# Reciprocals and scaling of attention outputs moved from VectorE to GpSimd in 14 of 16 chunks

## The chip, the cores and the metric

The kernel runs on one core of a Trainium2 chip. The metric is device time of the whole kernel in microseconds (us), as the median of several runs. The engines are TensorE (PE; PEld is its weight load), VectorE (DVE), ScalarE (ACT) and GpSimd (POOL); SyncE (SP) issues nearly all DMAs.

## What is computed

The reference is a transformer block with self-attention, cross-attention and a gated feed-forward part, followed by one more attention over the same context. Cut to what matters:

```python
def sdpa(q, k, v):
    probs = jax.nn.softmax(jnp.einsum('bid,bjd->bij', q, k) * SCALE, axis=2)
    return jnp.einsum('bij,bjd->bid', probs, v)

x = attention(ln32(x, ln1_s, ln1_b), ln32(x, ln1_s, ln1_b), Wq1, Wkv1, Wo1, bo1) + x
x = attention(ln32(x, ln2_s, ln2_b), context, Wq2, Wkv2, Wo2, bo2) + x
x = geglu_ff(ln32(x, ln3_s, ln3_b), Wff1, bff1, Wff2, bff2) + x
# second block: softmax((x Wq + bq)(ctx Wk + bk)^T) (ctx Wv + bv) + x
```

x is 4 x 1024 x 256 in float32, the context 4 x 154 x 256; there are 16 heads of 16 columns. Both multi-head attentions divide each head's output by the sum of its exponentials, and this division is what the change is about.

## The kernel before

**Tiling.** The 4096 rows are cut into 16 chunks of 256 (CH). A chunk passes through the stages `pre` (first normalisation, q, k, v), the self-attention (scores, maxima, exponentials, values), `mid` (output projection of the self-attention, residual, second normalisation, q of the cross-attention), `cross` (cross-attention) and `last` (output projection of the cross-attention, residual, third normalisation, feed-forward, final attention, store). The stages work on different chunks at the same time: body n of the main loop runs `pre` of chunk n, `mid` of chunk n - 6, `cross` of n - 7 and `last` of n - 8 beside the self-attention.

**Order.** Every engine has its own program, written as Python generators. The table ORDERS holds one string of letters for each body, and `walk` (L483) goes through it on every engine: each letter takes the next step of one stage or of the attention. All engines so walk the same list of steps; a step issues what that engine does in it, often nothing. Engines work in order and meet through semaphores, so an instruction that waits holds up everything behind it on its engine. The letter `i` stands for the reciprocal of a `last` chunk.

**The division.** The attention's values carry a column of ones, so each head's 17th row of output is the sum of its exponentials. Outputs and sums go to DRAM. In `mid` and in `last` the same six steps follow:

1. SP fetches the sums of 16 heads x 256 rows in packed form into den_c, 128 x 32 (load_den, L685; semaphore c_den).
2. DVE makes their reciprocals in place (invert, L1282; c_rd).
3. SP waits for c_rd and stores them to DRAM (store_inv, L689).
4. SP loads them back, each broadcast over the 16 rows of its head, into den, 128 x 512 (load_inv, L698). The unscaled outputs were loaded into oT before (load_sums, L693).
5. DVE multiplies oT by den in place (norm_o, L1287; c_on).
6. PE waits for c_on and projects (project_rows, L1560), DVE adds the residual (L1293).

Index 0 of these semaphores is `mid`, index 1 `last`. In the trace the second set of tiles carries the same names oT, den, x and xb.

**Work around it.** DVE's largest part is the maxima of the scores, 1024 reductions of 128 x 512 out of PSUM (L1398). In the feed-forward part DVE makes a gate from two SBUF tiles (L1356) and the hidden tile from it (L1359), which PE multiplies next (L1725). POOL makes the reciprocal square roots of the normalisations (L905, L907, an addition and a power with a tile of -0.5, 128 x 2), splits q and k into bfloat16 parts (L914, L916, L918, 128 x 512) and adds biases to the residuals (L935). At the start of `last`, POOL's bias addition to xb waits until the output of the chunk before is stored (c_outst).

Of the kernel before, what the change touches and what calls it, by code (L numbers as in the profile page):

```python
# [8 lines left out]
ALU = mybir.AluOpType  # L9
# [3 lines left out]
P = 128  # L13
B, S, D = 4, 1024, 256
H, DH = 16, 16
# [4 lines left out]
CH = 256  # L20
TT = CH // P
NCH = B * S // CH
# [16 lines left out]
EXPS2 = [name for name in ORDER2 if name[0] != "V"]  # L39
NE2 = len(EXPS2)  # L40
PR = 5
VSLOTS = 2
EPS = 1e-5
SCALE = 64 ** -0.5
# [125 lines left out]
def xattn_kernel(nc, t, out):  # L170

    ctx = ExitStack()
    with ctx:
        def sb(name, shape, dt=F32):
            return ctx.enter_context(nc.sbuf_tensor(name, shape, dt))
# [4 lines left out]
        def sem(name):  # L180
            return ctx.enter_context(nc.semaphore(name))
# [14 lines left out]

        ident = sb("ident", [P, P])
        neghalf = sb("neghalf", [P, TT])
        wq1 = sb("wq1", [P, KD, D])
        wkv1 = sb("wkv1", [P, KD, 2 * D])  # L200
        wo1 = sb("wo1", [P, KD, D])
# [44 lines left out]
        oT = sb("oT", [P, KD, CH])  # L246
        den = sb("den", [P, KD, CH])
# [28 lines left out]
        den_c = [sb(f"den_c{i}", [P, H * CH // P]) for i in range(2)]  # L276
# [68 lines left out]

        s_vec = sem("setup_vectors_loaded")
        s_load = sem("setup_pre_loaded")
        s_load2 = sem("setup_context_loaded")
        s_load3 = sem("setup_rest_loaded")
        s_const = sem("setup_constants")  # L350
# [63 lines left out]
        c_in = sem("mid_in_loaded")  # L414
# [4 lines left out]
        c_den = [sem(f"{c}_den_loaded") for c in ("mid", "last")]  # L419
        c_rd = [sem(f"{c}_inv_den") for c in ("mid", "last")]  # L420
# [429 lines left out]
        def _(pool):  # L850
            nc.gpsimd.memset(ident[:, :], 0.0).then_inc(s_const, 1)
            pool.wait_ge(s_const, 1)
            nc.gpsimd.affine_select(out=ident[:, :], in_=ident[:, :], compare_op=ALU.not_equal, fill=1.0, base=0,
                                    pattern=[[-1, P]], channel_multiplier=1).then_inc(s_const, 1)
            nc.gpsimd.memset(neghalf[:, :], -0.5).then_inc(s_const, 1)
            nc.gpsimd.memset(v_sb[:, :, :, DH:DH + 1], 1.0).then_inc(s_const, 1)
            nc.gpsimd.memset(head_v[1][:, :, :, DH:DH + 1], 1.0).then_inc(s_const, 1)
# [62 lines left out]
            def pre(p):  # L920
# [9 lines left out]
                for _ in range(2):  # L930
                    yield

            def add_bias(dst, x, bias, done):
                for i in range(TT):
                    last = nc.gpsimd.tensor_tensor(dst[:, i, :], x[:, i, :], bias[:, :], ALU.add)  # L935
                last.then_inc(done, 1)

            def mid(o, has_pre):
                yield
                pool.wait_ge(c_x0, (o + 1) * 16)  # L940
                add_bias(x0, x0, bo1, c_xb[0])
                for _ in range(3):
                    yield
                rstd(mv[0], ve[0], rs[0], c_mv[0], c_ve[0], c_rs[0], o + 1)
                for _ in range(3):
                    yield
                pool.wait_ge(c_q2st, o * 16)
                parts(q2_f, q2_parts, PART_AT[0], c_q2f, c_q2hi, c_q2rest, c_q2mid, c_q2lo, o + 1, o + 1)
                yield
                yield  # L950
# [5 lines left out]
            def last(o):  # L956
                e = last_set(o)
                if e == 0:
                    pool.wait_ge(c_outst, min(o, NCH - 2) * 16)
                else:  # L960
                    pool.wait_ge(g_o, NU)
                add_bias(xbs[e], x1[1 - (o + LAST_LAG) % 2], bo2, c_xb[1])
                for _ in range(4):
                    yield
                rstd(mv[1], ve[1], rs[1], c_mv[1], c_ve[1], c_rs[1], o + 1)
                yield
                pool.wait_ge(c_x[1], o + 1)
                add_bias(xbs[e], x2s[e], bff2, c_xb[2])
                for _ in range(LAST_STEPS - 5):
                    yield  # L970

            def body(n, flags):
                walk(n, setup_work, dict(pre=pre, mid=lambda o: mid(o, flags[0]), cross=cross, last=last), {}, seen)

            head()
            setup_work = setup()
# [223 lines left out]
        def _(dve):  # L1200
# [77 lines left out]

            def invert(which, o):

                dve.wait_ge(c_den[which], (o + 1) * 16)
                nc.vector.reciprocal(den_c[which][:, :], den_c[which][:, :]).then_inc(c_rd[which], 1)  # L1282

            def norm_o(which, sums, invs):

                o_flat = sums[:, :, :].rearrange("p k s -> p (k s)")
                nc.vector.tensor_tensor(o_flat, o_flat, invs[:, :, :].rearrange("p k s -> p (k s)"),  # L1287
                                        ALU.mult).then_inc(c_on[which], 1)
# [8 lines left out]
            def mid_by(u, has_last):  # L1297
                def mid(o, has_pre):
                    yield
                    invert(0, o)  # L1300
                    yield
                    yield
                    dve.wait_ge(c_in, (o + 1) * 64)
                    norm_o(0, oT, den)
                    yield
                    dve.wait_ge(c_wo[0], o + 1)
                    if has_last:
                        dve.wait_ge(c_xb[1], o - LAST_LAG + MID_LAG + 1)
                    residual(0, x1[u], ps_pre, x0, o)
                    stats(x1[u], st[0], mv[0], c_st[0], c_mv[0], o * 2)  # L1310
                    yield
                    dve.wait_ge(c_rs[0], o + 1)
                    normalise(den_rows, x1[u], mv[0], rs[0], c_xn[0])
                    for _ in range(4):
                        yield
                return mid
# [16 lines left out]
            def last(o):  # L1333
                e = last_set(o)
                bank_ = ps_lasts[e]
                yield
                yield
                dve.wait_ge(c_o2, (o + 1) * 64)
                norm_o(1, oT2s[e], den2s[e])
                yield  # L1340
                yield
                dve.wait_ge(c_wo[1], o + 1)
                residual(1, x2s[e], bank_, xbs[e], o)
                stats(x2s[e], st[1], mv[1], c_st[1], c_mv[1], o * 2)
                yield
                dve.wait_ge(c_rs[1], o + 1)
                normalise(oT2_rows_s[e], x2s[e], mv[1], rs[1], c_xn[1])
                yield
                dve.wait_ge(c_y3hi, o + 1)
                nc.vector.tensor_tensor(y3[1][:, :, :], den2s[e], y3[0][:, :, :].bitcast(F32),  # L1350
                                        ALU.subtract).then_inc(c_y3lo, 1)
                yield
                for m in range(FM):
                    dve.wait_ge(c_th, o * FM + m + 1)
                    dve.wait_ge(c_gb, o * FM + m + 1)
                    nc.vector.scalar_tensor_tensor(th[:, m % 2, :], th[:, m % 2, :], 1.0, gb[:, m % 2, :],  # L1356
                                                   ALU.add, ALU.mult).then_inc(c_gt, 1)
                    dve.wait_ge(c_gt, o * FM + m + 1)
                    nc.vector.scalar_tensor_tensor(hTs[e][:, m, :], last_banks(o)[m % 2][:, 0:CH], bff1[:, m:m + 1],  # L1359
                                                   th[:, m % 2, :], ALU.add, ALU.mult).then_inc(c_h, 1)  # L1360
                    yield
                for _ in range(4):
                    yield
                dve.wait_ge(c_f2, o + 1)
                residual(2, x2s[e], bank_, xbs[e], o)
                yield
                yield
                dve.wait_ge(c_s3, o + 1)
                for i in range(TT):
                    scores3 = bank_[:, i * CH:i * CH + CTX]  # L1370
                    nc.vector.tensor_tensor_reduce(scores3, scores3, m3_b[:, :], 1.0, -3.0e38, ALU.add, ALU.max,
                                                   accum_out=mx3[:, i:i + 1]).then_inc(c_mx3, 1)
                dve.wait_ge(c_mx3, (o + 1) * TT)
                nc.vector.tensor_scalar(nm3[:, :], mx3[:, :], -1.0, None, ALU.mult).then_inc(c_nm3, 1)
                yield
                dve.wait_ge(c_e3, (o + 1) * TT)
                dve.wait_ge(c_out, o * TT)
                nc.vector.reciprocal(inv3[:, :], sum3[:, :]).then_inc(c_inv3, 1)
                yield
                yield  # L1380
                dve.wait_ge(c_inv3, o + 1)
                dve.wait_ge(c_av3, o + 1)
                for i in range(TT):
                    nc.vector.scalar_tensor_tensor(xbs[e][:, i, :], bank_[:, i * D:(i + 1) * D], inv3[:, i:i + 1],
                                                   x2s[e][:, i, :], ALU.mult, ALU.add).then_inc(c_out, 1)
                yield
                yield
# [465 lines left out]
```

## Time and profile before

| | |
|---|---|
| median of 3 runs | 1559.94 us (1559.12 to 1562.54) |
| the profiled execution | 1565.36 us |
| its span in the trace | 1563.5 us |
| PE busy | 1499.9 us, 96% |
| DVE busy | 1107.8 us, 71% |
| ACT busy | 946.5 us, 61% |
| POOL busy | 253.7 us, 16% |

The span runs from the first to the last instruction, and 1.9 us of the execution lie around it. PE counts as busy while a matmul is in flight, and the ends of matmuls are modelled; a stretch in which the weight load (PEld) stands idle while a matmul drains shows only there. The time that an engine stood idle before an instruction is put down to whatever ended the wait last.

### The profile page before, as it was taken

The numbers are of one execution on the slowest core, as the hardware profiler recorded it, in microseconds if no ns is written. First come the engines' busy times: TensorE is split into PE (matmuls) and PEld (weight loads), VectorE is DVE, ScalarE is ACT, GpSimd is POOL, SyncE is SP. The second block draws the span as 40 slices with busy tenths as digits, with TensorE's granted clock in tenths as the row PEclk, the third lists the DMA queues.
The fourth block names the chain that finished last, engine by engine and source line by source line (L and its number), as shares of the span: only waits on it lengthen the run. The fifth ranks groups of instructions, "written<-read, shape, count | busy, mean of one in ns | idle before, by whom it ended". The sixth has DMA issues, their size and how long they took to land.

```text
span 1563.5 us, 44474 instructions
## 1 busy us (share of the span) xinstructions
PE 1499.9 (96%) x18122; PEld 1012.7 (65%) x18122; DVE 1107.8 (71%) x2269; ACT 946.5 (61%) x1928; POOL 253.7 (16%) x347
## 2 busy tenths in 40 slices
PE   6899999999999999999999999999999999998897
PEld 5555545675766767576766757666666757675676
DVE  4477787868678686767768586877778696863543
ACT  4366777656656575575666566665656566674343
POOL 2210322111202111121211212101101010002110
PEclk9899999999999999999999999999999999999999
DMA  8823453465242342527333262435423151413210
GB/s 225 198 72 110 137 104 90 103 126 116 66 99 67 94 91 70 117 62 151 77 92 76 75 122 68 105 72 106 98 61 90 27 120 49 99 51 88 59 36 14
DMA packets 228865, 143.93 MB, mean 92 GB/s; under 512 B 92787, under 2 KB 220597, under 8 KB 228405
## 3 DMA queue, kind: packets, MB, share of 16 engines
q1 hardware_dynamic: 228597, 141.07, 38.5%
q8 instruction: 143, 2.34, 0.7%
q14 instruction: 61, 0.50, 0.1%
q10 hardware_dynamic: 64, 0.02, 0.0%
HBM read 92.68 MB, written 47.74 MB: 90 GB/s over the span
## 4 chain that ended last, share of the span: by engine, by line
PE 78%; DVE 10%; DMA 4%; SPq 3%; ACT 2%; issue 2%; POOL 0%; DVEq 0%; POOLq 0%; ACTq 0%
PE ps_o L1806 12%; PE ps_last L1714 11%; PE ps_last L1725 7%; PE ps_max L1438 6%; PE ps_s L1438 6%; PE ps_max L1441 5%; PE ps_s L1441 5%; PE ps_pre L1551 4%; PE ps_pre L1560 4%; DVE mxh L1398 3%; DMA den<-o_s 2%; PE ps_cross L1652 2%; PE ps_cross L1656 2%; PE ps_last L1560 2%; PE ps_last L1756 1%
## 5 line engine op out<-in xcount | busy, mean ns | idle before, releaser
L1398 DVE TENSOR_REDUCE mxh<-ps_max 128x1 f32<-128x512 f32 x1024 | 657.8, 683 | 109.9 <-PE ps_max L1441 72.1
L1181 ACT ACTIVATE probs<-ps_s 128x512 f32<-128x512 f32 x1024 | 572.9, 598 | 221.4 <-PE ps_s L1441 112.0
L1806 PE MATMUL ps_o<-probs,vg 128*17 128x256 f32 x4096 | 295.8, 382 | 0.2 <-ACT o_sb L1187 0.2
L1438 PE MATMUL ps_max<-kst,qst 96*32 96x512 bf16 x2156 | 198.6, 384 | 3.1 <-DVE mxh L1398 0.8
L1438 PE MATMUL ps_s<-qst,kst 98*32 98x256 bf16 x4448 | 198.5, 274 | 1.8 <-issue 1.5
L1441 PE MATMUL ps_max<-kst,qst 96*128 96x512 bf16 x485 | 159.3, 382 | 10.2 <-DVE mxh L1398 6.5
L1438 PEld LDWEIGHTS ps_s<-qst,kst 98*32 98x32 bf16 x4448 | 116.6, 96 | 78.8 <-ACT probs L1181 15.0
L1356 DVE SCALAR_TENSOR_TENSOR th<-th,gb 128x256 f32<-128x256 f32 x128 | 58.8, 459 | 151.6 <-ACT gb L1156 151.3
L1441 PE MATMUL ps_s<-qst,kst 98*128 98x256 bf16 x936 | 158.3, 273 | 1.1 <-ACT probs L1181 0.4
L1806 PEld LDWEIGHTS ps_o<-probs,vg 128*17 128x17 f32 x4096 | 99.7, 97 | 79.0 <-issue 32.4
L1714 PE MATMUL ps_last<-y_hi,wff_hi 128*128 128x256 f32 x448 | 139.7, 312 | 5.5 <-DVE hT L1359 3.6
L1714 PE MATMUL ps_last<-y_lo,wff_hi 128*128 128x256 f32 x448 | 126.3, 282 | 0.0
L1714 PE MATMUL ps_last<-y_hi,wff_lo 128*128 128x256 f32 x448 | 126.0, 281 | 0.0
L1725 PE MATMUL ps_last<-wff,hT 128*128 128x256 f32 x480 | 115.4, 387 | 0.4 <-DVE hT L1359 0.4
L1154 ACT ACTIVATE th<-ps_last,b_tanh 128x256 f32<-128x256 f32 x112 | 53.0, 474 | 96.8 <-PE ps_last L1714 96.5
L1132 ACT ACTIVATE probs<-ps_cross 128x512 f32<-128x512 f32 x140 | 84.5, 603 | 44.1 <-PE ps_cross L1441 37.0
L1441 PEld LDWEIGHTS ps_s<-qst,kst 98*128 98x128 bf16 x936 | 82.2, 98 | 40.7 <-ACT probs L1181 10.1
L1438 PEld LDWEIGHTS ps_max<-kst,qst 96*32 96x32 bf16 x2156 | 57.9, 95 | 71.9 <-DVE mxh L1398 48.2
L1725 PEld LDWEIGHTS ps_last<-wff,hT 128*128 128x128 f32 x480 | 90.5, 193 | 16.8 <-DVE hT L1359 1.7
L1714 PEld LDWEIGHTS ps_last<-y_hi,wff_hi 128*128 128x128 f32 x448 | 84.8, 189 | 25.6 <-DVE hT L1359 16.0
L914 POOL TENSOR_TENSOR qk_f<-qk_f,qk_parts 128x512 f32<-128x512 f32 x40 | 46.4, 1159 | 302.5 <-ACT qk_f L1107 158.3
L1714 PEld LDWEIGHTS ps_last<-y_lo,wff_hi 128*128 128x128 f32 x448 | 85.3, 190 | 0.6
(278 smaller groups left out, 2110.2 us busy)
## 6 DMA issues: line engine op xcount, KB each, us to landing
vg<-v_s SPq DMA_DIRECT2D x64, 272.0 KB, 3.6
parts_s<-qk_parts SPq DMA_DIRECT2D x28, 384.0 KB, 4.3
o_s<-o_sb SPq DMA_DIRECT2D x64, 128.0 KB, 2.0
o_s<-o_sb SPq DMA_DIRECT2D x32, 256.0 KB, 2.5
oT<-o_s SPq DMA_DIRECT2D x62, 128.0 KB
den<-o_s SPq DMA_DIRECT2D x62, 128.0 KB
q_s<-qk_parts SPq DMA_DIRECT2D x16, 384.0 KB, 2.5
q2st<-q_s SPq DMA_DIRECT2D x16, 384.0 KB, 5.5
```

Source lines behind the costliest of these rows:

```text
L1132: nc.scalar.activation(tile, cross_banks[spare][x % 2][:, :], ACT.Exp, scale=SCALE).then_inc(c_e, 1)
L1154: nc.scalar.activation(th[:, m % 2, :], bank[:, CH:2 * CH], ACT.Tanh, scale=GELU_A / 2, bias=b_tanh[:, m:m + 1]).then_inc(c_th, 1)
L1181: nc.scalar.activation(probs[:, step % PR, 2 * pair:2 * pair + 2, :].rearrange("p j q -> p (j q)"), ps_s[pair][:, :], ACT.Exp, scale=SCALE ...
L1356: nc.vector.scalar_tensor_tensor(th[:, m % 2, :], th[:, m % 2, :], 1.0, gb[:, m % 2, :], ALU.add, ALU.mult).then_inc(c_gt, 1)
L1398: nc.vector.tensor_reduce(mxh[:, i % PAIRS, i // PAIRS:i // PAIRS + 1], ps_max[i % 2][:, :], AX_X, ALU.max).then_inc(g_mx, 1)
L1438: last = mm(bank[j * W:(j + 1) * W, cols_], keys[:, j * W:(j + 1) * W], queries, start=True, stop=True, tile_position=(0, j * W))
L1441: last = mm(bank[:, cols_], keys, queries, start=True, stop=True)
L1551: last = mm(bank[:, m * CH:(m + 1) * CH], w[:, k, m * P:(m + 1) * P], y[:, k, :], start=(k == 0), stop=(k == KD - 1))
L1560: last = mm(bank[:, i * D:(i + 1) * D], y[:, k, i * P:(i + 1) * P], w[:, k, :], start=(k == 0), stop=(k == KD - 1))
L1714: last = mm(last_banks(o)[m % 2][:, part * CH:(part + 1) * CH], wff1[w][:, k, cols_], y3[y][:, k, :], start=(i == 0), stop=(i == len(terms ...
L1725: last = mm(bank_[:, i * D:(i + 1) * D], hTs[e][:, m, i * P:(i + 1) * P], wff2[:, m, :], start=(m == 0), stop=(m == FM - 1))
L1806: last = mm(ps_o[j * W:j * W + VW, 0:CH], vg[:, unit % VSLOTS, kt, j * VW:(j + 1) * VW], probs[:, step % PR, j, :], start=(kt == 0), stop= ...
```

## The change

For the chunks 0 to 13 (POOL_NORMS = NCH - 2) steps 2 and 5 move from DVE to POOL. The reciprocal becomes a power with a tile of -1 (negone, 128 x 32), the multiplication is the same on POOL. The chunks 14 and 15 stay on DVE. The steps in which they are issued are the same letters of ORDERS. The waits go with them: POOL now waits for c_den and for c_in or c_o2. SP and PE wait for the same semaphores as before.

On DVE, around the multiplication of `mid` chunk 5 (th and hT are the gate and the hidden tile of `last`, mxh the maxima, x_0 the residual), before:

```order
L1356 SCALAR_TENSOR_TENSOR th<-th,gb 128x256
L1359 SCALAR_TENSOR_TENSOR hT<-ps_last,cols,th 128x256
L1398 TENSOR_REDUCE mxh<-ps_max 128x1 x6
L1287 TENSOR_TENSOR oT<-oT,den 128x512
L1293 TENSOR_TENSOR x_0<-ps_pre,x 128x512
L1259 BN_STATS st<-x_0 128x6 x2
L1262 BN_AGGR mv<-st 128x2 x2
```

and after:

```order
L1386 SCALAR_TENSOR_TENSOR th<-th,gb 128x256
L1389 SCALAR_TENSOR_TENSOR hT<-ps_last,cols,th 128x256
L1428 TENSOR_REDUCE mxh<-ps_max 128x1 x6
L1325 TENSOR_TENSOR x_0<-ps_pre,x 128x512
L1284 BN_STATS st<-x_0 128x6 x2
L1287 BN_AGGR mv<-st 128x2 x2
```

The multiplication is gone from between the maxima and the residual.

On POOL, at the start of `last` chunk 7 (qk_parts are the bfloat16 parts of q, xb with bo is the bias addition that waits for the output store, ve and rs belong to the normalisation behind the residual), before:

```order
L916 CAST qk_parts<-qk_f 128x512
L918 TENSOR_TENSOR qk_parts<-qk_f,qk_parts 128x512
L935 TENSOR_TENSOR xb<-x_0,bo 128x256 x2
L905 TENSOR_SCALAR ve<-mv 128x2
L907 TENSOR_TENSOR rs<-ve,neghalf 128x2
L935 TENSOR_TENSOR xb<-x,bff 128x256 x2
```

and after:

```order
L920 CAST qk_parts<-qk_f 128x512
L922 TENSOR_TENSOR qk_parts<-qk_f,qk_parts 128x512
L941 TENSOR_TENSOR den_c<-den_c,negone 128x32
L953 TENSOR_TENSOR xb<-x_0,bo 128x256 x2
L948 TENSOR_TENSOR oT<-oT,den 128x512
L909 TENSOR_SCALAR ve<-mv 128x2
L911 TENSOR_TENSOR rs<-ve,neghalf 128x2
L953 TENSOR_TENSOR xb<-x,bff 128x256 x2
```

The power stands ahead of the bias addition, and the multiplication between it and the normalisation.

On POOL, in `mid` chunk 8 (the second of two sets of parts of `pre`, then the normalisation of `mid`), before:

```order
L914 TENSOR_TENSOR qk_f<-qk_f,qk_parts 128x512
L916 CAST qk_parts<-qk_f 128x512
L918 TENSOR_TENSOR qk_parts<-qk_f,qk_parts 128x512
L905 TENSOR_SCALAR ve<-mv 128x2
L907 TENSOR_TENSOR rs<-ve,neghalf 128x2
```

and after:

```order
L918 TENSOR_TENSOR qk_f<-qk_f,qk_parts 128x512
L920 CAST qk_parts<-qk_f 128x512
L922 TENSOR_TENSOR qk_parts<-qk_f,qk_parts 128x512
L948 TENSOR_TENSOR oT<-oT,den 128x512
L909 TENSOR_SCALAR ve<-mv 128x2
L911 TENSOR_TENSOR rs<-ve,neghalf 128x2
```

The multiplication comes behind the parts. The diff, cut to its core (NCH is 16, H * CH // P is 32):

```diff
+POOL_NORMS = NCH - 2
...
+        negone = sb("negone", [P, H * CH // P])
...
+            nc.gpsimd.memset(negone[:, :], -1.0).then_inc(s_negone, 1)
...
+            def invert(which, o):
+                if o < POOL_NORMS:
+                    pool.wait_ge(s_negone, 1)
+                    pool.wait_ge(c_den[which], (o + 1) * 16)
+                    nc.gpsimd.tensor_tensor(den_c[which][:, :], den_c[which][:, :], negone[:, :], ALU.pow
+                                            ).then_inc(c_rd[which], 1)
+
+            def norm_o(which, sums, invs, o):
+                if o < POOL_NORMS:
+                    pool.wait_ge((c_in, c_o2)[which], (o + 1) * 64)
+                    o_flat = sums[:, :, :].rearrange("p k s -> p (k s)")
+                    nc.gpsimd.tensor_tensor(o_flat, o_flat, invs[:, :, :].rearrange("p k s -> p (k s)"),
+                                            ALU.mult).then_inc(c_on[which], 1)
...
             def mid(o, has_pre):
                 yield
+                invert(0, o)
                 pool.wait_ge(c_x0, (o + 1) * 16)
                 add_bias(x0, x0, bo1, c_xb[0])
...
+                norm_o(0, oT, den, o)
...
                 add_bias(xbs[e], x1[1 - (o + LAST_LAG) % 2], bo2, c_xb[1])
...
+                norm_o(1, oT2s[e], den2s[e], o)
...
             def invert(which, o):
 
+                if o < POOL_NORMS:
+                    return
+                dve.wait_ge(c_rd[which], o)
                 dve.wait_ge(c_den[which], (o + 1) * 16)
                 nc.vector.reciprocal(den_c[which][:, :], den_c[which][:, :]).then_inc(c_rd[which], 1)
```

## Rows read from the trace of the kernel before

**Rows 1.** The page: busy time of each engine, and the chain by engine.

```profile
PE 1499.9 (96%) x18122; PEld 1012.7 (65%) x18122; DVE 1107.8 (71%) x2269; ACT 946.5 (61%) x1928; POOL 253.7 (16%) x347
...
PE 78%; DVE 10%; DMA 4%; SPq 3%; ACT 2%; issue 2%; POOL 0%; DVEq 0%; POOLq 0%; ACTq 0%
```

**Rows 2.** Groups by line and shape: busy us, mean ns | idle before, releaser.

```profile
L1356 DVE SCALAR_TENSOR_TENSOR th<-th,gb 128x256 f32<-128x256 f32 x128 | 58.8, 459 | 151.6 <-ACT gb L1156 151.3
L1287 DVE TENSOR_TENSOR oT<-oT,den 128x512 f32<-128x512 f32 x31 | 21.6, 696 | 6.6 <-DMA den<-o_s 6.6
L1282 DVE RECIPROCAL den_c<-den_c 128x32 f32<-128x32 f32 x32 | 11.0, 343 | 8.7 <-DMA den_c<-o_s 8.7
...
L914 POOL TENSOR_TENSOR qk_f<-qk_f,qk_parts 128x512 f32<-128x512 f32 x40 | 46.4, 1159 | 302.5 <-ACT qk_f L1107 158.3 <-ACT qk_f L1085 144.2
L907 POOL TENSOR_TENSOR rs<-ve,neghalf 128x2 f32<-128x2 f32 x34 | 24.1, 709 | 2.8
L905 POOL TENSOR_SCALAR ve<-mv 128x2 f32<-128x2 f32 x34 | 8.1, 237 | 452.3 <-DVE mv L1262 452.3
```

**Rows 3.** Groups of L1560 on PE: projections of `mid` (ps_pre) and `last` (ps_last).

```profile
L1560 PEld LDWEIGHTS ps_pre<-wo,oT 128*128 128x128 f32 x128 | 23.3, 190 | 6.5 <-issue 3.7
L1560 PEld LDWEIGHTS ps_last<-wo,oT 128*128 128x128 f32 x120 | 22.7, 199 | 10.4 <-DVE oT L1287 7.3
...
L1560 PE MATMUL ps_last<-wo,oT 128*128 128x256 f32 x120 | 31.1, 404 | 4.6 <-DVE oT L1287 4.5
```

**Rows 4.** Waits: us in total, times, longest us.

```profile
SPq L689 <- DVE den_c L1282: 90.6, 21, 11.2
...
DVE oT L1287 <- DMA den<-o_s: 6.6, 6, 2.7
```

**Rows 5.** Timeline, `mid` of chunk 5, SP and DVE: start us, duration us.

```profile
571.84 0.57 SPq L685 DMA_DIRECT2D den_c<-o_s  x1
...
583.32 0.34 DVE L1282 RECIPROCAL den_c<-den_c 128x32 f32<-128x32 f32 x1
585.16 0.43 DVE L1356 SCALAR_TENSOR_TENSOR th<-th,gb 128x256 f32<-128x256 f32 x1 [1.50 <-ACT gb L1156]
...
601.15 1.26 SPq L698 DMA_DIRECT2D den<-o_s  x2
...
611.74 0.68 DVE L1287 TENSOR_TENSOR oT<-oT,den 128x512 f32<-128x512 f32 x1
614.62 0.69 DVE L1293 TENSOR_TENSOR x<-ps_pre,x 128x512 f32<-128x512 f32 x1 [2.20 <-PE ps_pre L1560]
```

**Rows 6.** Timeline, `last` of chunk 7 (912 to 916) and chunk 9.

```profile
912.02 0.34 DVE L1282 RECIPROCAL den_c<-den_c 128x32 f32<-128x32 f32 x1
912.35 3.41 SPq L749 DMA_DIRECT2D v2b<-v_s  x4
915.80 0.59 SPq L689 DMA_DIRECT2D o_s<-den_c  x1
...
1088.06 0.35 DVE L1282 RECIPROCAL den_c<-den_c 128x32 f32<-128x32 f32 x1
...
1094.90 1.27 SPq L698 DMA_DIRECT2D den<-o_s  x2
...
1102.56 0.69 DVE L1287 TENSOR_TENSOR oT<-oT,den 128x512 f32<-128x512 f32 x1 [1.54 <-DMA den<-o_s]
1103.31 1.38 PEld L1560 LDWEIGHTS ps_last<-wo,oT 128*128 128x128 f32 x7 [1.79 <-DVE oT L1287]
```

**Rows 7.** Timeline, POOL instructions beside DVE's gate (L1356).

```profile
409.54 1.16 POOL L918 TENSOR_TENSOR qk_parts<-qk_f,qk_parts 128x512 bf16<-128x512 f32 x1
409.63 1.35 DVE L1356 SCALAR_TENSOR_TENSOR th<-th,gb 128x256 f32<-128x256 f32 x1 [1.52 <-ACT gb L1156]
...
486.37 0.70 POOL L907 TENSOR_TENSOR pre_rs<-pre_ve,neghalf 128x2 f32<-128x2 f32 x1
486.69 0.41 DVE L1356 SCALAR_TENSOR_TENSOR th<-th,gb 128x256 f32<-128x256 f32 x1
```

More of the change, by code:

```diff
@@ L347, in xattn_kernel @@
         s_load = sem("setup_pre_loaded")
+        s_negone = sem("setup_negone_set")
         s_load2 = sem("setup_context_loaded")
@@ L939, in mid @@
                 yield
+                invert(0, o)
                 pool.wait_ge(c_x0, (o + 1) * 16)
                 add_bias(x0, x0, bo1, c_xb[0])
-                for _ in range(3):
-                    yield
+                yield
+                yield
+                norm_o(0, oT, den, o)
+                yield
                 rstd(mv[0], ve[0], rs[0], c_mv[0], c_ve[0], c_rs[0], o + 1)
@@ L962, in last @@
                 add_bias(xbs[e], x1[1 - (o + LAST_LAG) % 2], bo2, c_xb[1])
-                for _ in range(4):
-                    yield
+                yield
+                yield
+                norm_o(1, oT2s[e], den2s[e], o)
+                yield
+                yield
                 rstd(mv[1], ve[1], rs[1], c_mv[1], c_ve[1], c_rs[1], o + 1)
@@ L972, in body @@
             def body(n, flags):
-                walk(n, setup_work, dict(pre=pre, mid=lambda o: mid(o, flags[0]), cross=cross, last=last), {}, seen)
+                walk(n, setup_work, dict(pre=pre, mid=lambda o: mid(o, flags[0]), cross=cross, last=last),
+                     dict(i=lambda o: invert(1, o)), seen)
             head()
@@ L1279, in invert, with norm_o @@
             def invert(which, o):
+                if o < POOL_NORMS:
+                    return
+                dve.wait_ge(c_rd[which], o)
                 dve.wait_ge(c_den[which], (o + 1) * 16)
                 nc.vector.reciprocal(den_c[which][:, :], den_c[which][:, :]).then_inc(c_rd[which], 1)
-            def norm_o(which, sums, invs):
+            def norm_o(which, sums, invs, o):
+                if o < POOL_NORMS:
+                    return
+                dve.wait_ge(c_on[which], o)
+                dve.wait_ge((c_in, c_o2)[which], (o + 1) * 64)
                 o_flat = sums[:, :, :].rearrange("p k s -> p (k s)")
@@ L1302, in mid @@
                     yield
-                    dve.wait_ge(c_in, (o + 1) * 64)
-                    norm_o(0, oT, den)
+                    norm_o(0, oT, den, o)
                     yield
@@ L1337, in last @@
                 yield
-                dve.wait_ge(c_o2, (o + 1) * 64)
-                norm_o(1, oT2s[e], den2s[e])
+                norm_o(1, oT2s[e], den2s[e], o)
                 yield
```

## The prediction

> **What bounds the kernel now.** I read the busy shares and the chain first [rows 1]: TensorE (PE) is busy for 96% of the span and carries 78% of the chain that ended last, VectorE (DVE) is busy for 71% and carries 10%. PE is the bound, and time taken from DVE counts only where PE stands waiting for DVE. Next I read what the moved work costs on either engine [rows 2], and how PE stands before the two projections that read its result [rows 3]: 7.3 and 4.5 us, 11.8 in all, are waits for the multiplication (L1287) in the `last` stage, and next to nothing in `mid`. No compute engine waits for the reciprocals (L1282). Then the queues [rows 4]: SyncE (SP) stood 90.6 us, in 21 pieces, before the store of the reciprocals, because DVE came to them late. Then one or two chunks of each stage in the timeline [rows 5, 6], and last the places where an instruction of GpSimd (POOL) and one of DVE meet [rows 7].
>
> **What leaves DVE.** 28 reciprocals of 0.343 us and 28 multiplications of 0.69 us: 9.6 + 19.4 = 29 us of 1107.8 [rows 1, 2]. At full value that would be 29 us; the timeline allows far less. In `mid` chunk 5 DVE makes the reciprocal at 583.32, and before its next instruction it stands idle for 1.50 us until ScalarE has delivered; it ends the multiplication at 612.42 and stands idle for 2.20 us until PE has projected [rows 5]. All 14 `mid` multiplications look like that, and behind 23 of the 28 reciprocals DVE runs idle before PE has waited for anything queued after them. The other five could return up to 0.34 us each; I take 1.3 us together. Behind the `last` multiplication DVE has a queue of 3 to 10 us of maxima, which PE waits for in some chunks; there 0.69 us less is worth about 2 us over 14 chunks. Bounds for the relief are 0 and 5 us; I take 3.3.
>
> **What POOL pays.** The POOL row of the multiplication's shape (L914, two float32 inputs, 128x512) is 1.16 us against 0.69 on DVE, 0.47 more. The power on 128x32 is in no row. The nearest is the same operation on 128x2, 0.71 us, where a plain POOL instruction of that size takes 0.24 [rows 2]. Sixteen times the elements can't cost less than 0.71. If the whole difference of 0.47 us belongs to two elements, one costs 0.236, and 32 cost 0.24 + 7.55 = 7.8 us. So it lies between 0.71 and 7.8. Some of the 0.47 us must be a start that is paid once, and a loop over 32 can overlap what one over two can't, so the value lies nearer to the measured row; I take 2 us. POOL has room: it is busy for 254 us of 1563 [rows 1], and 28 x (2 + 1.16) = 88 us come on top.
>
> **`mid`.** In chunk 5 the den is fetched at 571.84, DVE inverts it 11.5 us later, the broadcast load is issued at 601.15, and DVE multiplies at 611.74 [rows 5]. In all 14 chunks DVE comes to the multiplication 1.5 to 15 us after its data have landed, so POOL, idle then, ends it earlier in each, and a power of up to 7.8 us still ends about when the late reciprocal did. What is gained is PE's wait: 6.5 us idle before this projection's weight loads over 16 chunks, 3.7 of it not put down to any producer [rows 3], so at most 2.8 x 14/16 = 2.5 us. Matmuls still in flight cover part of that; I take 1.5. The next late thing is PE's own queue. SP is free earlier, but no row shows PE or ScalarE waiting for a load that is queued behind this store, so I give nothing for it. On POOL the bias addition to x0 stands behind the power; its reader is the residual after the projection, tens of us later.
>
> **`last`.** This stage can lose. In chunk 9 the broadcast lands at 1102.56, after 1.54 us of idle DVE, and PE has stood 1.79 us when it starts at 1103.31 [rows 6]. Six times DVE waited for that load, 6.6 us in all [rows 4], once in an unchanged chunk; there PE gets the result 0.47 us later. With the chunks where DVE came late by less than that, seven lose 0.2 to 0.47 us: 2.7 us. The power adds to it only where its result is waited for at once. In chunk 7 the reciprocal is done at 912.36, and SP stores it only at 915.80, behind other loads; in chunk 9 it is done at 1088.41, and SP issues the broadcast at 1094.90, behind other stores [rows 6]. A power of 2 us therefore shows in two chunks (1 and 5), 1.6 us more; one of 4 us costs 7 more than the 2.7, one of 7.8 us reaches nearly all 14 with 2 to 7 us each, 40 more. Four chunks (2, 6, 10, 13), where DVE was the late one, gain 0.2 to 0.4 us each, 1.3 us. On POOL the multiplication stands behind the bias addition to xb, which waits for the store of the output before; in three chunks (2, 3, 8) that addition ends about when the broadcast has landed or up to 2.8 us after, still early enough to lose under 0.5 us, which is among the seven. Together: 2.7 + 1.6 - 1.3 = +3 us.
>
> **The shared port.** When POOL's subtraction had started at 409.54, DVE's gate with two inputs (L1356) of 409.63 took 1.35 us, where the mean is 0.46 [rows 2, 7]. POOL's `mid` multiplications now fall where DVE makes gates: by the landing times four of 28 meet one, at about 0.5 us, 2 us. The bounds are 0 and 28 x 0.9 = 25 us; I take 2. The power of 0.70 us at 486.37 has a gate that started inside it and took 0.41 us [rows 7], and two others of the 48 powers read alike, so I charge nothing for a power. The Trainium skill (SBUF — State Buffer, section Who interferes with whom) says that a DVE instruction with two SBUF inputs and a GpSimd one that reads SBUF exclude each other for the whole instruction. By that rule the first meeting is as it should be, and the one inside a power is not; it is rival (b). The Trainium skill (GPSIMD Engine Reference, section When to use GPSIMD) advises against elementwise work with two inputs on this engine, as about 2 times slower. The rows here give 1.7 times, and by 2 times `last` would lose about 1 us more.
>
> **The sum.** -3.3 (relief) - 1.5 (`mid`) + 3 (`last`) + 2 (port) = +0.2 us. The profiled execution took 1565.36 us, 5.4 above the median of 1559.94; the change leaves it at 1565.6 and the median at 1560. With a power of 0.71 us the sum is 1.6 us less, with one of 3 us 2.3 more. A measurement of this kernel tells 0.2%, 3.1 us, from no change: faster is below 1556.8, slower above 1563.1.
>
> **Rivals.** (a) Slower: the power costs by the element. It decides from about 3.5 us on, where the road of the den becomes later than SP and DVE were. At 4 us `last` loses 2.7 + 7 - 1.3 = 8.4, total +5.6, 1565; at 7.8 us it loses 43, total +40, 1600. For it: 0.24 us an element is what the rows give if nothing is overhead. Against it: a price read off two elements tells little of a loop. (b) Slower by the port: the power holds it while it computes. DVE makes 128 gates [rows 2], 0.08 in a us, so 28 x 2 us of powers meet five, at about 1 us each, and PE waits for what follows a gate: +5, 1565; with a power of 7.8 us it would be 18 meetings of 4 us, 70 us. The gates that started inside powers speak against it. (c) Faster: the relief is worth its 5 us, all of `mid`'s 2.5 comes, a power of 0.71 us costs `last` 1.4 net and the meetings cost nothing: -6, 1554. For it: 29 us of DVE work are gone. Against it: the idle time that follows each piece.
>
> **How the numbers follow.** The forecast (a power of up to 3.5 us) gets 0.60 and gives 1556 to 1563: 0.43 of it within 0.2%, 0.08 faster, 0.09 slower. Rival (a) with 3.5 to 5.5 us gets 0.10 (1563 to 1575), above that 0.15 (1575 to 1600); (b) 0.05; (c) 0.10. That is faster 0.18, same 0.43, slower 0.39. From 1555 to 1590 leaves out half of (c), the longest powers and part of (b), under 0.2. The likeliest case's own range is 1556 to 1563.
>
> **What would show it.** First the mean of the 28 powers on 128x32. DVE's busy time should fall by 29 us; SP's 90.6 us before the store should shrink to under 30. The idle time before `mid`'s weight loads should fall, that before those of `last` rise from 10.4 by 1 to 3 us; 20 would be rival (a). A mean of the gates above 0.46 us would show the port. The forecast is wrong if the power takes over 3.5 us, or if PE was paced by DVE's maxima over longer stretches than those I followed.

## The result: 1607.56 us, 3.1% slower

Three runs of the changed kernel have a median of 1607.56 us (1607.07 to 1610.89) beside 1559.94: a ratio of 1.0307, interval 1.0279 to 1.0336. The prediction was 1560.0, range 1555 to 1590, with 0.39 for slower. The time lies beyond the range, on the side of rival (a). The profiled execution took 1610.89 us with a span of 1609.0, 45.5 us more than before (1563.5).

In the changed kernel the power stands in line 941, POOL's multiplication in 948, what DVE keeps of both in 1310 and 1319, the projection in 1590, and SP's store and broadcast load in 692 and 701. The page of the changed kernel, its busy times and its chain by engine, beside [rows 1]:

```profile
PE 1516.6 (94%) x18122; PEld 1022.9 (64%) x18122; DVE 1085.2 (67%) x2213; ACT 947.2 (59%) x1928; POOL 440.2 (27%) x404
...
PE 70%; DMA 10%; POOL 7%; DVE 5%; SPq 3%; ACT 2%; issue 2%; POOLq 0%; DVEq 0%; ACTq 0%
```

The durations of DVE's instructions fall by 28.9 us in sum, as forecast (its busy time, in which neighbours overlap, by 22.6), and the span grows by 45.5. POOL goes from nothing to 7% of the chain, DMA from 4 to 10%: the road of the denominators (load, invert, store, broadcast load, multiply) has come onto the path. PE is busy 16.7 us longer with the same 18122 instructions.

The groups by line and shape of the changed kernel (busy us, mean ns | idle before, releaser), beside [rows 2, 3]:

```profile
L941 POOL TENSOR_TENSOR den_c<-den_c,negone 128x32 f32<-128x32 f32 x28 | 152.6, 5449 | 170.2 <-DMA den_c<-o_s 170.2
...
L948 POOL TENSOR_TENSOR oT<-oT,den 128x512 f32<-128x512 f32 x28 | 35.8, 1278 | 118.1 <-DMA den<-o_s 113.4 <-DMA oT<-o_s 4.7
...
L911 POOL TENSOR_TENSOR rs<-ve,neghalf 128x2 f32<-128x2 f32 x34 | 24.3, 716 | 2.8
...
L1386 DVE SCALAR_TENSOR_TENSOR th<-th,gb 128x256 f32<-128x256 f32 x128 | 60.2, 470 | 153.8 <-ACT gb L1181 153.5
...
L1590 PEld LDWEIGHTS ps_last<-wo,oT 128*128 128x128 f32 x120 | 28.7, 251 | 38.9 <-POOL oT L948 33.3 <-DVE oT L1319 0.7
...
L1590 PEld LDWEIGHTS ps_pre<-wo,oT 128*128 128x128 f32 x128 | 24.5, 198 | 15.9 <-issue 12.7
```

The first row is the miss: a power on 128x32 took 5.45 us, not 2. The two last rows are where it is paid: idle time before the projection's weight loads goes from 10.4 to 38.9 us in `last` and from 6.5 to 15.9 in `mid` [rows 3], 37.9 us together. The 12.7 us that the last row puts down to "issue" are mostly waits for POOL's multiplication, read from the times: in the largest the weight load starts 0.1 us after that multiplication ends (chunk 0, below). The gate's mean went from 459 to 470 ns, 1.4 us over 128: the port is not where the time went. A gate that ran wholly inside a power (986.48 to 992.09, shown below for chunk 9) took as long as the 81 beside no POOL instruction (0.425 us in the mean):

```profile
990.05 0.42 DVE L1386 SCALAR_TENSOR_TENSOR th<-th,gb 128x256 f32<-128x256 f32 x1 [2.24 <-ACT gb L1181]
```

The waits (us, times, longest), beside [rows 4]:

```profile
SPq L692 <- POOL den_c L941: 144.4, 22, 18.9
...
SPq L692 <- DVE den_c L1310: 12.9, 4, 5.0
```

SP was to stand there under 30 us; it stands 157 in place of 90.6.

The waits of `last` chunks 4, 10 and 13 in the changed kernel (in brackets, us):

```profile
671.32 2.63 PEld L1590 LDWEIGHTS ps_last<-wo,oT 128*128 128x128 f32 x7 [5.29 <-POOL oT L948]
...
1225.27 1.59 PEld L1590 LDWEIGHTS ps_last<-wo,oT 128*128 128x128 f32 x8 [3.42 <-POOL oT L948]
...
1484.05 3.06 PEld L1590 LDWEIGHTS ps_last<-wo,oT 128*128 128x128 f32 x8 [4.42 <-POOL oT L948]
```

The granted clock there, in windows of the span (us, then the busy time of PE, PEld, DVE, ACT and POOL, the clock, the DMA share, GB/s). The first piece holds the wait of chunk 4, the second begins 0.7 us before its end, the third holds the wait of chunk 13:

```profile
660.00:670.00 10.00, 6.25 (x106) 3.09 (x100) 7.35 (x14) 5.01 (x10) 1.41 (x2) 1.00 0.43 133
670.60:677.40 6.80, 6.08 (x27) 4.35 (x31) 2.15 (x8) 0.00 (x0) 0.99 (x3) 0.50 0.28 60
...
1476.10:1493.10 17.00, 11.01 (x79) 5.49 (x78) 7.30 (x16) 2.83 (x6) 7.76 (x11) 0.50 0.34 102
```

From about the end of the wait on TensorE is granted half its clock, 1.2 GHz. In the kernel before, where this projection starts at 657.50, the stretch behind it has 1.00:

```profile
656.70:663.50 6.80, 6.79 (x91) 4.36 (x88) 6.66 (x18) 3.91 (x8) 2.03 (x4) 1.00 0.41 89
```

It falls in the same way at the waits of `last` chunks 1, 5, 8, 9, 12 and 13 and of `mid` chunk 0. It does not fall at every such wait: behind the 3.42 us of `last` chunk 10 and the 2.1 to 2.2 us of `last` chunk 0 and `mid` chunks 7 and 9 it stays at 1.00. The 17 us of the third piece also hold a stretch of cross-attention scores in which the kernel before is at half clock for 6.8 us. The mean clock falls from 0.988 to 0.972 (0.977 and 0.979 in the other two runs). Since the low level is half the high one, 0.972 and 0.988 are about 2 x 0.028 x 1609 = 90 us at half clock in place of 2 x 0.012 x 1563.5 = 38.

### The profile page after: what moved, and what is told of

It is laid out like the page before. It is cut to its first block, busy times and chain, and to the rows that moved or that the text cites. A ratio compares the mean times of both kernels' runs of the same rounds, so it can differ in the third digit from the quotient of the medians.

```text
span 1609.0 us, 44511 instructions
## 1 busy us (share of the span) xinstructions
PE 1516.6 (94%) x18122; PEld 1022.9 (64%) x18122; DVE 1085.2 (67%) x2213; ACT 947.2 (59%) x1928; POOL 440.2 (27%) x404
## 3 DMA queue, kind: packets, MB, share of 16 engines
q8 instruction: 143, 2.34, 0.6%
## 4 chain that ended last, share of the span: by engine, by line
PE 70%; DMA 10%; POOL 7%; DVE 5%; SPq 3%; ACT 2%; issue 2%; POOLq 0%; DVEq 0%; ACTq 0%
PE ps_last L1744 10%; PE ps_o L1836 10%; PE ps_last L1755 7%; PE ps_max L1471 5%; PE ps_s L1468 5%; PE ps_max L1468 5%; PE ps_s L1471 5%; PE ps_pre L1581 4%; POOL den_c L941 4%; PE ps_pre L1590 3%; DMA den<-o_s 3%; PE ps_last L1590 3%; DMA den_c<-o_s 2%; DMA o_s<-o_sb 2%; PE ps_cross L1682 2%
## 5 line engine op out<-in xcount | busy, mean ns | idle before, releaser
L941 POOL TENSOR_TENSOR den_c<-den_c,negone 128x32 f32<-128x32 f32 x28 | 152.6, 5449 | 170.2 <-DMA den_c<-o_s 170.2
```

The costliest lines, as they stand in the source:

```text
L941: nc.gpsimd.tensor_tensor(den_c[which][:, :], den_c[which][:, :], negone[:, :], ALU.pow).then_inc(c_rd[which], 1)
```

## Experiments

**The theories.** A: the length of the power, on the denominators' road, is the loss. B: the move itself is, by POOL's order, the slower multiplication or the port. Ratios are to the kernel before, run beside each on the same chip; the waits are the idle time before the weight loads of the two projections, as in the rows above, and the clock is the mean granted, both of the profiled execution.

| run | on POOL | ratio (95%) | `last` waits | `mid` waits | clock |
|---|---|---|---|---|---|
| before | nothing | 1 | 10.4 | 6.5 | 0.988 |
| changed | power 5.45 us, scaling | 1.0307 (1.0279-1.0336) | 38.9 | 15.9 | 0.972 |
| e1_product | product 0.27 us, scaling | 1.0027 (1.0013-1.0041) | 9.0 | 11.6 | 0.988 |
| e11_quarter_power | 1.91 us, scaling | 1.0083 (1.0066-1.0099) | 15.2 | 12.1 | 0.983 |
| e6_half_power | 3.15 us, scaling | 1.0116 (1.0096-1.0135) | 22.4 | 12.3 | 0.985 |
| e2_scaling_only | scaling | 1.0044 (1.0026-1.0063) | 9.8 | 11.7 | 0.987 |
| e3_reciprocal_only | power | 1.0184 (1.0166-1.0201) | 27.7 | 10.1 | 0.982 |
| e4_mid_only | both, `mid` | 1.0068 (1.0046-1.0089) | 8.5 | 16.5 | 0.986 |
| e5_last_only | both, `last` | 1.0202 (1.0185-1.0219) | 38.7 | 6.5 | 0.979 |
| e12_mid_free | both, ten chunks of `mid` | 1.0010 (0.9998-1.0022) | 10.4 | 6.0 | 0.988 |
| e8_no_first | scaling, not `mid` 0, 1 | 1.0000 (0.9987-1.0012) | 12.0 | 5.9 | 0.986 |
| e9_filler | as changed | 1.0259 (1.0240-1.0278) | 19.5 | 14.7 | 0.987 |
| e10_before_filled | nothing | 0.9981 (0.9966-0.9996) | 8.1 | 6.5 | 0.992 |

### The power's length: e1, e11, e6

```diff
-  nc.gpsimd.tensor_tensor(den_c[which][:, :], den_c[which][:, :], negone[:, :], ALU.pow
+  nc.gpsimd.tensor_tensor(den_c[which][:, :], den_c[which][:, :], negone[:, :], ALU.mult
...
```

> The changed kernel, with the power of 128x32 in 14 chunks replaced by a multiplication of the same tiles (so the outputs are scaled by the negated denominators, not divided: the time alone is of interest). Everything else, the place on POOL and the slower multiplication of 128x512, stays. Theory A (the 5.45 us of the power, on the way from the denominators to the projection, are the loss): a multiplication of 128x32 should take under 1 us, as the two-column power (0.71) bounds it, so at most 14 x 2 x 0.3 us remain in place of 14 x 2 x 5.1, and the time is 1556 to 1563 us. Theory B (the move itself is the loss: POOL takes its work in order, and the step stands behind the means and variances of the next projection, or the multiplication takes 1.28 in place of 0.70 us): the time stays at 1595 to 1608 us.

1.0027: 4 us of the 48 are left, just above A's range and far from B's. What is left is in `mid`, 5.1 us more of waits there and 1.4 less in `last`. Nearly all of it stands in one place. POOL in `mid` of chunk 0 of the changed kernel (timeline: start, us), where the same 4.93 us appear, and the projection behind it:

```profile
175.61 1.16 POOL L918 TENSOR_TENSOR qk_f<-qk_f,qk_parts 128x512 f32<-128x512 f32 x1 [0.62 <-ACT qk_f L1110]
176.83 0.61 POOL L920 CAST qk_parts<-qk_f 128x512 bf16<-128x512 f32 x1
177.52 1.16 POOL L922 TENSOR_TENSOR qk_parts<-qk_f,qk_parts 128x512 bf16<-128x512 f32 x1
178.64 1.27 POOL L902 TENSOR_TENSOR wff_lo<-hT,wff_hi 128x512 fp32r<-128x512 f32 x1
183.65 2.48 POOL L902 TENSOR_TENSOR wff_lo<-hT,wff_hi 128x512 fp32r<-128x512 f32 x2 [3.74 <-ACT wff_hi L1087]
186.09 1.26 POOL L948 TENSOR_TENSOR oT<-oT,den 128x512 f32<-128x512 f32 x1
...
187.47 2.63 PEld L1590 LDWEIGHTS ps_pre<-wo,oT 128*128 128x128 f32 x7 [4.93 <-issue]
```

POOL takes its work in order. Ahead of the multiplication stands the splitting of weights (L902), which waits 3.74 us for ScalarE; the multiplication follows it at once and PE waits 4.93 us. In the kernel before DVE did it at 183.62:

```profile
183.62 0.68 DVE L1287 TENSOR_TENSOR oT<-oT,den 128x512 f32<-128x512 f32 x1
```

The two shorter powers, e6 with a half (and e11 with `// 4` in place of `// 2`):

```diff
-  nc.gpsimd.tensor_tensor(den_c[which][:, :], den_c[which][:, :], negone[:, :], ALU.pow
+  w = H * CH // P // 2
+  nc.gpsimd.tensor_tensor(den_c[which][:, 0:w], den_c[which][:, 0:w], negone[:, 0:w], ALU.pow)
+  nc.gpsimd.tensor_tensor(den_c[which][:, w:], den_c[which][:, w:], negone[:, w:], ALU.mult
...
```

> The changed kernel with the power on 16 of the 32 columns, and a multiplication on the other 16 (half of the denominators are not inverted; the time alone is of interest). If a power costs by the column, (5.45 - 0.71) / 30 = 0.158 us each, this one takes about 2.9 us and the multiplication 0.2 to 0.4. The prediction's threshold of about 3.5 us says that this length still hides: 1558 to 1565 us. If the loss grows in proportion to the length from the start: 1580 to 1590 us.

> The changed kernel with the power on 8 of the 32 columns and a multiplication on the other 24 (three quarters of the denominators are not inverted; the time alone is of interest). The powers of 128x2, 128x16 and 128x32 took 0.72, 2.92 and 5.43 us, 0.157 us more for each column; 128x8 should then take 1.66 us and the step with its multiplication 1.9 us, which is about the 2 us that the prediction took for a power. If only that price was wrong, the prediction's sum holds here: 0.998 to 1.003. If something else in the sum was wrong too (the wait of chunk 0 of `mid`, 4.9 us in each run with that multiplication on POOL, and the slack of `last`): 1.003 to 1.008.

Groups of e6 and then of e11, the power and the projection of `last`:

```profile
L942 POOL TENSOR_TENSOR den_c<-den_c,negone 128x16 f32<-128x16 f32 x28 | 81.7, 2918 | 171.6 <-DMA den_c<-o_s 171.6
...
L1592 PEld LDWEIGHTS ps_last<-wo,oT 128*128 128x128 f32 x120 | 24.1, 211 | 22.4 <-POOL oT L950 17.8 <-DVE oT L1321 1.2
```

```profile
L942 POOL TENSOR_TENSOR den_c<-den_c,negone 128x8 f32<-128x8 f32 x28 | 46.6, 1663 | 172.5 <-DMA den_c<-o_s 172.4
...
L1592 PEld LDWEIGHTS ps_last<-wo,oT 128*128 128x128 f32 x120 | 23.8, 208 | 15.2 <-POOL oT L950 10.9 <-DVE oT L1321 1.0
```

The price is a straight line: 0.716, 1.663, 2.918 and 5.449 us for 2, 8, 16 and 32 columns, 0.40 + 0.157 a column (the first is the power of the normalisations, with an exponent of -0.5). The loss begins far below the prediction's 3.5 us: it is 0.8% at 1.91 us and 1.2% at 3.15 (1580.0 us). It is no straight line either: 1.9 of the 3.1% come between 3.15 and 5.45 us, so a bend near 3.5 us is not excluded. The waits of `last` rise by 3.8, 5.8 and 7.2 us for each further us, as more chunks lose their slack: 3, 6, 8 and 9 of the 14 have over 1 us of idle time before their weight loads at 0.27, 1.91, 3.15 and 5.45 us. At 3.15 us the loss is neither hidden, as the forecast had it, nor quite in proportion to the length. At about the prediction's own 2 us (1.91) the kernel was 13 us slower, so the price is not the only term that failed.

### One half of the change each: e2, e3

```diff
             def invert(which, o):
-                if o < POOL_NORMS:
+                if o < 0:
```

The line is changed so on both engines for the reciprocal (e2), and in the same way for the multiplication (e3).

> Half of the change: the 28 multiplications of 128x512 on POOL, all 32 reciprocals on DVE. Theory A: each multiplication is 0.58 us longer, two in a row before a chunk's projection, against 16.5 to 20 us less of DVE work: 1557 to 1564 us. Theory B (POOL's order and the slower multiplication): 1585 to 1608 us.

> The other half: the 28 reciprocals as powers on POOL, all 64 multiplications of 128x512 on DVE. Theory A: the loss is all here, 1598 to 1608 us. Theory B: half the loss or less, 1560 to 1585 us.

In e3 DVE makes 32 multiplications, not the 64 of its expectation. Scaling alone costs 0.4%, a little over A's range, with a wait as long as the 4.93 us of chunk 0 in it. Reciprocals alone cost 1.8%, between the two theories: A's "all here" falls. The halves sum to 2.3%, under the whole 3.1%. `last` shows why: alone, the longer multiplication leaves its waits at 9.8 us (10.4 before); on top of the power it takes them from 27.7 to 38.9, and 14 x 0.58 us are 8.1 of that. This fits a slack that hides the longer multiplication alone and is used up once the power stands ahead of it.

### One stage each, and the free chunks: e4, e5, e8, e12

```diff
             def invert(which, o):
-                if o < POOL_NORMS:
+                if which == 0 and o < POOL_NORMS:
```

This is e4, in all four places (both steps, on both engines; e5: `which == 1`).

> The change in `mid` alone (14 powers and 14 multiplications on POOL), `last` as before. In the changed kernel's profile the projections of `mid` waited 12.9 us in place of 4.0, in chunks 0, 1, 7 and 9, where the power or the multiplication stood behind the work that POOL does for the next projection. Theory A (each lengthening shows where it is waited for): 4 to 14 us over before, ratio 1.003 to 1.009. The prediction's claim that nothing is lost in `mid` gives 0.998 to 1.001. If the two places only hurt together (a late `mid` makes `last` late): under 1.003 here and under 1.015 in `last` alone.

> The change in `last` alone, `mid` as before. In the changed kernel the projections of `last` waited 34.0 us in place of 7.7, and TensorE was granted its lower clock behind several of these waits. Theory A: 26 us of waits and 6 to 10 us of clock, ratio 1.020 to 1.024. The waits alone, without the clock: 1.015 to 1.018. The two halves should sum to the whole change (1.031) if they are independent.

1.0068 and 1.0202: `last` carries three quarters of their sum and `mid` a quarter, and within the intervals the sum, 2.7%, is the whole. In `mid`, chunk 9 of the changed kernel shows the second way to lose there:

```profile
984.67 0.61 POOL L920 CAST qk_parts<-qk_f 128x512 bf16<-128x512 f32 x1
985.36 1.16 POOL L922 TENSOR_TENSOR qk_parts<-qk_f,qk_parts 128x512 bf16<-128x512 f32 x1
986.48 5.61 POOL L941 TENSOR_TENSOR den_c<-den_c,negone 128x32 f32<-128x32 f32 x1
992.05 1.42 POOL L953 TENSOR_TENSOR x<-x,bo 128x256 f32<-128x256 f32 x2
1000.36 1.26 POOL L948 TENSOR_TENSOR oT<-oT,den 128x512 f32<-128x512 f32 x1 [6.88 <-DMA den<-o_s]
...
1001.74 1.59 PEld L1590 LDWEIGHTS ps_pre<-wo,oT 128*128 128x128 f32 x8 [2.19 <-issue]
```

The denominators had landed 32.9 us earlier. The power stands behind the parts of `pre` of a later chunk, runs as soon as they are done, and PE waits 2.19 us for what follows. Two runs leave such chunks out:

```diff
+MID_FREE = (2, 3, 4, 5, 6, 8, 10, 11, 12, 13)
-                if o < POOL_NORMS:
+                if which == 0 and o in MID_FREE:
```

> The change in `mid` alone, and there only in the ten chunks (2 to 6, 8, 10 to 13) whose projection waited no longer in the changed kernel than before; the others as before. If the loss in `mid` comes only from the chunks where POOL holds other work ahead of the power or the multiplication (0, 1, 7, 9), a power of 5.45 us is hidden in these ten: 0.998 to 1.001. If the powers cost in `mid` wherever they stand: 1.003 to 1.006.

1.0010 (0.9998 to 1.0022): ten powers of 5.45 us are hidden or nearly so. The loss in `mid` comes from chunks 0, 1, 7 and 9, where other work stands ahead on POOL. Order alone does it in chunks 0 and 1; in 7 and 9 it takes the power's length as well, for with the 0.27 us product in the same places (e1) the idle time there is 0.20 and 0.17 us in place of 2.29 and 2.34. In e8 every reciprocal is on DVE, and so are the multiplications of `mid` chunks 0 and 1, as well as those of chunks 14 and 15:

```diff
             def norm_o(which, sums, invs, o):
-                if o < POOL_NORMS:
+                if (which == 1 or o >= 2) and o < POOL_NORMS:
```

> Only multiplications on POOL, all in `last` (0 to 13) and those of `mid` from chunk 2 on; every reciprocal on DVE. The run with all 28 multiplications on POOL lost 7 us, and its trace shows 4.9 us of that as one wait in `mid` of chunk 0, where POOL splits weights ahead of the multiplication. Theory A: without chunks 0 and 1 the loss is gone, and the relief of DVE is worth at most the 3.3 us that the prediction gave it: 0.998 to 1.001. If the longer multiplication itself costs (1.28 in place of 0.70 us, in 26 places): 1.002 to 1.005.

1.0000 (0.9987 to 1.0012). Without chunks 0 and 1 of `mid` the slower multiplication and the 13.7 us less of DVE's busy time (1107.8 to 1094.1) together make no difference that shows; what either is worth alone no run shows.

### The clock: e9 and e10

```diff
+FILLED = (1, 4, 5, 8, 9, 10, 12, 13)
...
-                pe.wait_ge(c_on[1], o + 1)
...
+                if o in FILLED:
+                    whole()
+                    for _ in range(6):
+                        mm(bank_[:, 0:D], wo2[:, 0, 0:P], wo2[:, 1, :], start=True, stop=True)
+                pe.wait_ge(c_on[1], o + 1)
```

> The changed kernel with six matmuls of 128x256 (0.4 us each, 2.4 us in all, their result overwritten by the projection) ahead of the wait for the scaled outputs, in the eight chunks of `last` whose projection waited 1.9 to 5.3 us. TensorE then works in the first half of each wait. If part of the loss is the lower clock that TensorE is granted behind these waits (1.2 in place of 2.4 GHz, 3.4 to 6.8 us at a time), 4 to 10 us come back: 0.993 to 0.997 of the changed kernel's time, 1.024 to 1.028 of the time before. If the waits alone are the loss: the time of the changed kernel or up to 5 us more, 1.030 to 1.034 of the time before.

1.0259 beside 1.0307: 7.5 us come back although PE has more to do; by the two intervals, which nearly touch, that is 2 to 13 us. Groups of e9, then its stretch beside the windows shown above (its projection of chunk 4 starts at 670.76):

```profile
L1731 PE MATMUL ps_last<-wo 128*128 128x256 f32 x96 | 24.2, 407 | 0.0
...
L1591 PEld LDWEIGHTS ps_last<-wo,oT 128*128 128x128 f32 x120 | 22.7, 197 | 19.5 <-POOL oT L949 11.9 <-issue 4.8
```

```profile
660.00:670.00 10.00, 8.21 (x106) 4.94 (x94) 6.72 (x13) 4.51 (x9) 1.96 (x3) 1.00 0.53 157
670.00:677.00 7.00, 6.18 (x87) 4.16 (x91) 4.10 (x11) 2.39 (x5) 2.98 (x5) 1.00 0.51 112
```

Filler and remaining waits of both stages are 24.2 + 19.5 + 14.7 = 58.4 us, 3.6 more than the 54.8 they replace, yet the time falls: the clock stays at 1.00 behind chunk 4, and its mean is 0.987 in place of 0.972 (over all their runs 0.981 to 0.987 and 0.972 to 0.979). The projection's weight loads are back at 197 ns from 251. So the lower clock behind the waits was worth about 7.5 + 3.6 = 11 us of the 48 (an estimate from these rows, as uncertain as the 7.5); with the waits' 37.9 that makes up the loss. That sum is a rough one: in e5 the waits rise by 28.3 us and the time by 31.5, which leaves 3 us for the clock there.

The kernel before has two stretches at half clock of its own, at the cross-attention scores of the last two chunks, where PE and DVE take turns. e10 fills them:

```diff
                         last.then_inc(c_mt, 1)
+                        if o >= NCH - 2:
+                            whole()
+                            for j in range(2 if f < 2 * Q2F - 1 else 8):
+                                mm(ps_cross[:, 0:CTX], q2st[0:ROWS, h0, i * P:(i + 1) * P],
+                                   k2st[0:ROWS, h0, 0:CTX], start=True, stop=True)
                         yield
```

> The kernel before (no work moved), with two matmuls of 128x154 behind each group of cross-attention scores of chunks 14 and 15, and eight behind the last group, their result overwritten: TensorE works while it waits for the maxima there. In the profile before it is granted 1.2 GHz for 6.8 us behind each of these two stretches (1436.5 and 1480.8 us). If filling short waits holds its clock up there as it did in the changed kernel, up to 6 us come back: 0.996 to 0.999, a kernel faster than both. If the clock falls for something else, or the matmuls make the groups later: 1.000 to 1.003.

0.9981 (0.9966 to 0.9996), 1556.75 us beside 1560.31: a small gain, with an interval that ends just under 1, and faster than both kernels. Windows of chunk 15, first of the kernel before, then of e10, which is there 6 us earlier:

```profile
1480.80:1487.60 6.80, 5.98 (x20) 4.18 (x19) 3.45 (x8) 0.00 (x0) 0.00 (x0) 0.50 0.24 74
```

```profile
1474.80:1481.60 6.80, 6.65 (x46) 5.37 (x46) 4.22 (x9) 0.00 (x0) 0.00 (x0) 1.00 0.20 64
```

The clock is at 1.00 there in place of 0.50, and at chunk 14 it is at half for 3.4 us (1435.0 to 1438.4) in place of 6.8; the mean is 0.992.

## Why the prediction was wrong

- **The power (taken at 2 us, bounds 0.71 and 7.8).** The first step that failed. The bounds held, the choice between them didn't: "the value lies nearer to the measured row" had no row behind it. Of the 0.47 us that two columns cost over a plain instruction, 0.31 belong to the columns (2 x 0.157) and 0.16 to the start, so the element's price was the better guide. The reason given, that a loop over 32 can overlap what one over two can't, is in no run: each further column cost the same 0.157 us. Rival (a) had the mechanism, with 0.25 in all for lengths over 3.5 us.
- **`mid` (-1.5 us).** Wrong in sign: +10.6 us in e4. "POOL, idle then" was read from chunk 5 and from POOL's low share (16%); in chunks 0, 1, 7 and 9 its queue held `pre`'s parts or the weights just then. The diff made the two new steps entries of an in-order queue, and what stands ahead of them there was not followed chunk by chunk. The 3.7 us that the row puts down to "issue" were read as no wait for a producer; in the changed kernel 12.7 us stand there, mostly waits for POOL.
- **`last` (+3 us at 2 us).** In waits nearly right at that length: +4.8 in e11 at 1.91 us. But rival (a) was to decide only from 3.5 us on; in the runs the waits grow from the shortest power on, and faster with each us. At 5.45 us they had grown by 28.5.
- **The clock.** In no term. About 11 us of the whole, by the estimate from e9.
- **The relief (-3.3 us).** No run has it by itself. With the longer multiplications it comes to nothing measurable (1.0000 in e8), and in e1, where all the work is off DVE, the loss left is about the one wait of chunk 0. Both fit its bounds of 0 and 5; its size stays open.
- **The port (+2 us).** +1.4 us by the mean of the gates, and four gates met a multiplication, as counted (0.42, 0.45, 0.57 and 1.22 us). Rival (b), with its meetings of a microsecond and more, is out: nine gates ran wholly inside a power and took 0.42 to 0.43 us. The rule from the Trainium skill (SBUF — State Buffer, Who interferes with whom) that two such instructions exclude each other is not what the runs show for a power.
- **POOL's multiplication (1.16 us).** 1.28 us measured, and the slack hid it where POOL was free.
- **"11.8 us in all".** The 7.3 and 4.5 us of [rows 3] are the same waits, once on the weight loads and once on the matmuls behind them, and don't add. Those who waited for line 948 in the changed kernel (us, times) show it again:

```profile
  PEld ps_last L1590: 33.3, 11
  PE ps_last L1590: 29.8, 10
```

With the power at 5.45 us, the method's own numbers (5.6 at 4 us, 40 at 7.8) give about 19 us by a straight line between them. (The 40 leaves out the gain of 1.3 us that the other sums have; with it 39.) Some 29 us were missing, above all the 10.6 of `mid` and the 11 of the clock, which overlap in part. Size and two mechanisms were off, not the size alone.

## What to carry to other kernels

An operation whose price is in no row at its size should be priced by the element as well as by the nearest row, and where the two differ tenfold the forecast should not rest on the cheap end. An engine with a low busy share is not free at a given moment: follow what stands ahead in its queue in every chunk, one-time work of the first chunks too. Where the bound engine is made to wait some microseconds, look at the granted clock behind the wait, and if nothing else can be done, measure what filling the wait with idle work gives.

## What the runs showed of the hardware

- A power of float32 on GpSimd took 0.40 + 0.157 us a column of 128 partitions (2 to 32 columns), where a multiplication of 128x32 took 0.27 us there and DVE's reciprocal of 128x32 0.34.
- DVE's two-input gates were not held up beside it: nine ran wholly inside a power and took 0.42 to 0.43 us, and all 128 took 470 ns in the mean with 153 us of powers on POOL, 459 before.
- The granted clock fell to 1.2 GHz at eight single waits of 1.9 to 5.3 us on PE, and did not at four of 2.1 to 3.4 us. It came back after 3.4 to 6.8 us, after 17 where a second stretch of waiting followed. 3 us of matmuls in such waits kept it at 2.4 GHz in most places, and 7.5 us came back in all (2 to 13 by the intervals).
